# Later scaling and splitting of the output weight, an earlier first output tile, and re-timed first loads and text logits in a two-layer cross-attention kernel

## The reference

```python
# layer 0
q = split(x @ Wq.T); k, v = split(text @ Wk.T), split(text @ Wv.T)
k_ip, v_ip = split(ip @ Wk_ip.T), split(ip @ Wv_ip.T)
out = merge(attend(q, k, v)) + merge(attend(q, k_ip, v_ip))
x = out @ Wo.T + bo + x
# layer 1: its own weights, and one more term in the image scores
text_probs = softmax((q @ k_text.T) * scale)
sem = ((text_probs @ text) @ ip.T) * scale
ip_probs = softmax(scores + 0.5 * sem) * mask
x = (text_out + ip_out) @ Wout + bout + x
```

## Time and profile before

| | |
|---|---|
| median of 3 runs | 1746.2 us (1746.16 to 1747.57) |
| the profiled execution | 1748.87 us, of it span 1747.1 us |
| PE, DVE, ACT, POOL busy | 99%, 71%, 45%, 25% |
| HBM traffic | 133.96 MB read, 60.88 MB written, 112 GB/s |

### The profile page before, as it was taken

One profiled execution on the slowest core, in us unless ns is written; L12 is line 12 of the kernel. 1 busy time (PEld: TensorE's weight loads), 2 busy tenths in 40 slices (PEclk: granted clock), 3 DMA queues, 4 the chain that ended last, 5 costly groups with the idle time before them and its releaser, 6 DMA issues.

```text
span 1747.1 us, 52495 instructions
## 1 busy us (share of the span) xinstructions
PE 1727.5 (99%) x22178; PEld 1405.7 (80%) x22178; DVE 1241.9 (71%) x3112; ACT 781.2 (45%) x1579; POOL 441.9 (25%) x543
## 2 busy tenths in 40 slices
PE   8999999999999999999999999999999999999998
PEld 4778888888888888887577888888888888888875
DVE  6877676767677777676845567767676767677686
ACT  3334555554545454545322344534353445345343
POOL 3034333333342424223200112212121212122111
PEclk9999999999999999999999999999999999999999
DMA  8653535343434343435146232423142323224212
GB/s 327 128 158 115 161 117 154 113 135 113 135 110 139 109 136 112 139 108 200 61 88 175 64 97 75 117 75 96 48 136 53 116 65 119 62 83 109 82 45 70
DMA packets 124450, 198.45 MB, mean 114 GB/s; under 512 B 41928, under 2 KB 111064, under 8 KB 117496
## 3 DMA queue, kind: packets, MB, share of 16 engines
q1 hardware_dynamic: 118888, 168.95, 33.5%
q10 hardware_dynamic: 5328, 26.15, 4.0%
HBM read 133.96 MB, written 60.88 MB: 112 GB/s over the span
## 4 chain that ended last, share of the span: by engine, by line
PE 92%; DVE 4%; DMA 2%; ACT 1%; issue 1%; POOL 0%; SPq 0%; ACTq 0%; DVEq 0%
PE proj L597 65%; PE pv L752 6%; PE st L729 5%; PE rows L709 4%; PE rows L597 3%; PE proj L545 3%; PE proj L586 2%; PE rows L710 2%; DMA arena<-k_dram 1%; DMA raw<-text_dram 1%; PE rows L797 1%; ACT arena L1149 0%; PE rows L760 0%; DVE wparts L1508 0%; PE pv L661 0%
## 5 line engine op out<-in xcount | busy, mean ns | idle before, releaser
L597 PE MATMUL proj<-w_hl,cbuf 128*128 128x128 f16 x9600 | 600.9, 219 | 0.0
L597 PE MATMUL proj<-cbuf,w_hl 128*128 128x322 f16 (+1 forms) x3840 | 591.5, 300 | 0.4 <-DVE arena L1760 0.3
L597 PEld LDWEIGHTS proj<-w_hl,cbuf 128*128 128x128 f16 x9600 | 548.7, 98 | 2.3 <-issue 0.3
L597 PEld LDWEIGHTS proj<-cbuf,w_hl 128*128 128x128 f16 x3840 | 367.6, 97 | 163.7 <-DVE arena L1760 0.6
L1411 POOL TENSOR_TENSOR arena<-arena 128x400 f16<-128x400 f32 x240 | 231.1, 963 | 860.2 <-ACT arena L1149 860.2
L1148 ACT ACTIVATE arena<-st,rs 128x400 f16<-128x400 f32 x480 | 287.1, 598 | 259.3 <-DVE st L1886 155.2
L1124 ACT ACTIVATE arena<-proj 128x323 f16<-128x323 f32 (+1 forms) x160 | 70.6, 441 | 487.8 <-PE proj L597 487.8
L1149 ACT ACTIVATE arena<-st,rs 128x400 f32<-128x400 f32 x480 | 286.0, 596 | 0.0
L1805 DVE TENSOR_TENSOR arena<-arena 128x400 f16<-128x400 f32 x240 | 147.3, 614 | 95.7 <-ACT arena L1149 92.6
L752 PEld LDWEIGHTS pv<-arena 128*128 128x128 f16 x3840 | 175.2, 97 | 22.0 <-POOL arena L1411 0.8
L752 PE MATMUL pv<-arena 128*128 128x34 f16 (+3 forms) x3840 | 192.4, 189 | 0.5 <-POOL arena L1411 0.5
(11 more groups left out here) (202 smaller groups left out, 1675.6 us busy)
## 6 DMA issues: line engine op xcount, KB each, us to landing
arena<-k_dram SPq DMA_DIRECT2D x240, 185.2 KB, 3.6
k_dram<-arena SPq DMA_DIRECT2D x160, 161.2 KB, 1.9
raw<-ctx_dram SPq DMA_DIRECT2D x16, 1290.0 KB, 7.8
c_dram<-cbuf SPq DMA_DIRECT2D x16, 1290.0 KB, 6.7
cbuf<-c_dram SPq DMA_DIRECT2D x14, 1290.0 KB, 8.0
cbuf<-w_dram ACTq DMA_DIRECT2D x24, 640.0 KB, 8.2
arena<-q_dram SPq DMA_DIRECT2D x48, 125.0 KB, 2.6
w_hl<-w_dram ACTq DMA_DIRECT2D x8, 640.0 KB, 12.5
```

The costliest lines, as they stand in the source:

```text
L597: mm = nc.tensor.matmul(out, x[a](k), w[b](k), start=(k == 0 and m == 0), stop=(k == KT - 1 and m == 2))
```

## The change

It has six parts. (1) For the output weight, DVE's `turned_max` stays in the window g = 1 of the last batch but moves ahead of the second semantic tile, and `scale_chain` moves behind `prob_low(u, 2)`. (2) ACT's high parts move from g = 1 and 2 to g = 2 and 3. DVE's low parts 0 and 1 are made in g = 2, 2 and 3 in g = 3, and 4 in the last window, g = 4. (3) `out_tile(l, 0, 0)` is evicted by DVE before the third row maximum instead of behind it; in the last window DVE evicts tile 1 behind `prob_low(u, 0)` and tile 2 before `add_semantic(u, 3)`. (4) In `last_window` PE does `weigh(u, 0)` before score tile 3, and `out_tile(l, 0, 3)` begins after it. (5) In the preamble of layer 1 PE does `k_part(STEPS + 1, 1)` before `logits(0)`; ACT and DVE follow. (6) x comes in two pieces, both on SP; ACT waits for the first before it issues the rest of its loads, and issues the second weight's load after four evictions instead of two.

```diff
@@ -45,7 +45,7 @@
 QW = QK * C
 CH = KT * IP // 2
 TH = KT * TW // 2
-X_PIECES = ((0, 2), (2, 4), (4, CT))
+X_PIECES = ((0, 2), (2, CT))
 CB = 10400
 ORDER = (0, 2, 1, 3)
 TAIL_BANKS = (0, 1, 4)
@@ -187,7 +187,7 @@
 
         const_in, ready, sel_in = sem("const_in"), sem("ready"), sem("sel_in")
         x_in, wq_first, wq_in, wo_in = (sem("x_in0"), sem("x_in1")), sem("wq_first"), sem("wq_in"), sem("wo_in")
-        x_piece = tuple(sem(f"x_piece{n}") for n in range(3))
+        x_piece = tuple(sem(f"x_piece{n}") for n in range(2))
         wq_last = sem("wq_last")
         text_in, t_parts, t_chain, t_high, t_scaled = ((sem("text_in0"), sem("text_in1")), sem("t_parts"), sem("t_chain"), sem("t_high"),
                                                        sem("t_scaled"))
@@ -466,7 +466,7 @@
                         sp.wait_ge(v_full, 2 * (LAYERS * STEPS - G))
                         sp.dma_start(wo_raw, wo_d[1]).then_inc(wo_in, 16)
 
-            for n, (a, b) in enumerate(X_PIECES[0:2]):
+            for n, (a, b) in enumerate(X_PIECES):
                 sp.dma_start(x_first[:, a:b], x_d[0][:, a:b]).then_inc(x_piece[n], 16)
             sp.dma_start(wq[:, 3:], wq_d[0][:, 3:]).then_inc(wq_last, 16)
             sp.dma_start(raw[:, 0:TH], text_d[:, 0:TH]).then_inc(text_in[0], 16)
@@ -821,11 +821,10 @@
                 score_tile(u, 1)
                 out_tile(l, 0, 2, range(3, CT))
                 score_tile(u, 2)
-                out_tile(l, 0, 3, range(2))
+                weigh(u, 0)
                 score_tile(u, 3)
                 o_turn(u - 1)
-                out_tile(l, 0, 3, range(2, 4))
-                weigh(u, 0)
+                out_tile(l, 0, 3, range(4))
                 score_tile(u, 4)
                 out_tile(l, 0, 3, range(4, CT)), out_tile(l, 0, 4, range(1))
                 weigh(u, 1)
@@ -984,9 +983,9 @@
                 bank_done(pe, "vt", 1, TT - 1, c)
                 k_part(STEPS, c, 0, KT)
             k_part(STEPS + 1, 0, 0, KT)
+            k_part(STEPS + 1, 1, 0, KT)
             pe.wait_ge(pads, 2)
             logits(0)
-            k_part(STEPS + 1, 1, 0, KT)
             text_ip(0)
             odd_part(1, range(KT // 2))
             turn_probs(0)
@@ -1186,7 +1185,7 @@
                 n, k = u + 1, u + 2
                 more, more2 = exists(n, l), exists(k, l)
                 splits = iter(SLICES[4 * (g - 1):4 * g] if l == 0 and i < B - 1 and g in (1, 2) else ())
-                chunks = iter(((0, 1, 2, 3), (4,))[g - 1] if i == B - 1 and g in (1, 2) else ())
+                chunks = iter(((0, 1, 2, 3), (4,))[g - 2] if i == B - 1 and g in (2, 3) else ())
 
                 def split():
                     for k in splits:
@@ -1230,14 +1229,13 @@
                     k_unit(k, 0)
 
             act.dma_start(wq[:, 0], wq_d[0][:, 0]).then_inc(wq_first, 16)
-            a, b = X_PIECES[2]
-            act.dma_start(x_first[:, a:b], x_d[0][:, a:b]).then_inc(x_piece[2], 16)
+            act.wait_ge(x_piece[0], 16)
             act.dma_start(wq[:, 1:3], wq_d[0][:, 1:3]).then_inc(wq_in, 16)
             act.dma_start(raw[:, TH:], text_d[:, TH:]).then_inc(text_in[1], 16)
             load_weight(0, 0)
             q_tile(0, 0, 0), q_tile(0, 0, 1)
+            q_tile(0, 0, 2), q_tile(0, 0, 3)
             load_weight(0, 1)
-            q_tile(0, 0, 2), q_tile(0, 0, 3)
             act.wait_ge(t_chain, 5)
             for k in range(4):
                 split_text(k)
@@ -1316,8 +1314,8 @@
                 bank_done(act, "vt", 1, TT - 1, c)
             q_split(B)
             k_unit(STEPS, 0), k_unit(STEPS, 1)
+            k_unit(STEPS + 1, 0), k_unit(STEPS + 1, 1)
             logits(0)
-            k_unit(STEPS + 1, 0), k_unit(STEPS + 1, 1)
             odd_unit(1)
             act.wait_ge(pads, 2)
             turn_semantic(0)
@@ -1634,7 +1632,6 @@
 
             def wo_scale(l):
 
-                turned_max(os, "wo", l)
                 scale_chain(os, o_chain, 5 * l, os[:, 4:5], os[:, 5:6])
                 dve.wait_ge(tops, 2 * B + 2 * l)
                 nc.vector.tensor_scalar(oscale[:], ounit[:], os[:, 5:6], None, ALU.mult).then_inc(o_units, 1)
@@ -1906,7 +1903,7 @@
                     for _, c in zip(range(1 if l and count < 8 else count), wo_parts):
                         wo_part(l, c)
 
-                chunks = iter(((0, 1), (2, 3))[g - 1] if i == B - 1 and g in (1, 2) else ())
+                chunks = iter((2, 3) if i == B - 1 and g == 3 else ())
 
                 def low():
                     for c in lows:
@@ -1926,7 +1923,8 @@
                     normalise(u - 1)
                 if not more:
                     add_semantic(u, 1)
-                    out_tile(l, 0, 1)
+                if g == 1 and i == B - 1:
+                    turned_max(os, "wo", l)
                 if l == 0 and g == 1 and i < B - 1:
                     context_scale(i + 1)
                 if l == 0 and g == 2 and i < B - 1:
@@ -1938,17 +1936,21 @@
                 if more:
                     add_semantic(u, 1)
                 prob_low(u, 0)
-                if g == 1 and i == B - 1:
-                    wo_scale(l)
                 if ahead and g == 4:
                     semantic(i + 1)
                 low()
                 context_work(2)
                 if not more:
+                    out_tile(l, 0, 1)
+                add_semantic(u, 2)
+                if not more:
                     out_tile(l, 0, 2)
-                add_semantic(u, 2)
                 add_semantic(u, 3)
                 prob_low(u, 2)
+                if g == 1 and i == B - 1:
+                    wo_scale(l)
+                if not more:
+                    wo_low(l, 4)
                 if ahead and g == 2:
                     text_probs(i + 1)
                 context_work(2)
@@ -1961,6 +1963,8 @@
                     out_tile(l, 0, 3)
                 add_semantic(u, 5)
                 low()
+                if g == 2 and i == B - 1:
+                    wo_low(l, 0)
                 sooner = l and not (ahead and g == 3)
                 if more and sooner:
                     maxima(n, 0)
@@ -1978,10 +1982,10 @@
                     maxima(n, 1)
                     if more2:
                         k_unit(k, 0)
+                    else:
+                        out_tile(l, 0, 0)
                     maxima(n, 2)
                     context_work(1)
-                    if not more2:
-                        out_tile(l, 0, 0)
                     maxima(n, 3)
                     shift_parts(n)
                 context_work(8)
@@ -1990,7 +1994,7 @@
                 if i == B - 1 and g == 0:
                     wo_max(l)
                 if i == B - 1 and g == 2:
-                    wo_low(l, 4)
+                    wo_low(l, 1)
                 if g == 1 and i < B - 1:
                     q_split(r + 1)
 
@@ -2142,10 +2146,10 @@
             layer_scale(1)
             all_scales()
             k_unit(STEPS, 1)
+            k_unit(STEPS + 1, 0)
+            k_unit(STEPS + 1, 1)
             logits(0)
-            k_unit(STEPS + 1, 0)
             text_probs(0)
-            k_unit(STEPS + 1, 1)
             text_ip(0)
             probs_put(0)
             semantic(0)
```

## The result

The changed kernel takes 1752.1 us (median of 13 runs, 1749.41 to 1756.73), the kernel before 1746.99 beside it (13 runs, 1746.16 to 1748.67): a ratio of 1.0028, 95% interval 1.0020 to 1.0035. The profiled execution took 1752.93 us, its span is 1751.1 us.

The account below looks back on a forecast made before the run. PE's matmuls were taken to bound the kernel (1727.5 us, 99% of the span), so only its waits could change. Gains of 0.7, 1.0 and 2.1 less losses of 2.7 and 0.95 gave 1746.1 us, range 1743.8 to 1748.6.

Parts of the forecast that it names:

- the late load: Last window of layer 0: next query weight's load issued later, takes 6.6 us; PE stands 2.7 us (1.9 to 4.4).
- the logits: Preamble of layer 1: 0.68 us wait covered, but text_ip starts later; 0.95 us lost (0.7 to 1.3).
- the start: First loads: SP's text half lands about 1 us sooner; 0.7 us gained (0.1 to 1.6).
- The gain in g = 1: Last batch, window g = 1: PE's waits shrink; 1.0 us gained in layer 0, 2.1 in layer 1.
- The rival that VectorE becomes the bound there: Window g = 1: scale chain holds PE's projection, half of the 3.1 us given back; 1747.6 us, chance 13%.
- Windows g = 2 and 3: Last batch, ACT's moved high parts: zero cost, at most 0.4 us lost per layer.
- the first output tile: Evicted a maximum sooner by DVE: no effect, 0.3 us either way for both layers.
- The last window of layer 1: PE's block 4 waits for the low part, weigh(u, 0) fills another wait: zero, 0.3 us either way.
- the load collides: Layer change: load takes 8.3 us beside weight loads, PE stands 4.4; 1747.8 us, 8%; with slow clock about 1750.2, 5%.
- nothing moves: Start: small DMAs eat the text's lead, so nothing is gained there; 1746.8 us, chance 15%.
- the signs that were to show the prediction right: Changed profile: g = 1 at 17.4 to 17.7 us, later wq load and wait, text_ip wait about 1.5, text before 15.6.

Follow-up runs that it names:

- a2: The kernel before with only the changed first loads (part 6): 1749.72 us, ratio 1.0011 to the kernel before.
- c2: The kernel before with one edit, low part 4 of the output weight made in the last window: 1753.76 us, ratio 1.0035.
- c3: The kernel before with part 5 alone, both key projection parts ahead of the text logits: 1749.54 us, ratio 1.0013.
- a1: The changed kernel with its first loads as they were before (part 6 undone): 1752.31 us, ratio 1.0023 to the kernel before.
- d1: Changed kernel, parts 5 and 6 undone, low parts 2 and 3 in VectorE's gap in g = 3, part 4 where 3 stood, both layers: 1744.49 us.
- a3: The changed kernel with the fifth low part right behind the fourth, in g = 3: 1749.21 us, ratio 1.0007 to the kernel before.
- c1: Changed kernel, parts 5 and 6 undone, in layer 0 alone the fifth low part behind the last row maximum of g = 3: 1746.17 us.
- d2: d1 with x_late issued ahead of the mask's row on SyncE's queue: 1744.58 us, ratio 0.9984 to the kernel before.
- e1: d1 with layer 1's low parts where the changed kernel has them, so the gap is used in layer 0 alone: 1744.55 us, ratio 0.9982.
- c4: The changed kernel with SyncE's half of the text issued only when wq blocks 1 and 2 have landed: 1756.42 us, ratio 1.0055.
- a4: The changed kernel with the second key projection behind the logits again (part 5 undone): 1751.77 us, ratio 1.0021 to the kernel before.
- b2: The changed kernel with 16 dummy matmuls ahead of the wait for layer 1's query weight: 1753.02 us, ratio 1.0031 to the kernel before.
- b1: The changed kernel with 15 dummy matmuls after the first query tile at the start: 1751.66 us, ratio 1.0023 to the kernel before.
- b4: The changed kernel without ACT's wait for the first piece of x: 1753.79 us, ratio 1.0033 to the kernel before.

## Why the prediction was wrong

By the experiments, the sum should have read: start +1.6 (a2), g = 1 -1.14 and -2.35, the late load +6.0 (c2), the logits +1.7 (c3), g = 3 of layer 1 +0.3. That is 6.1, against 5.1 measured by the medians; the parts' runs agree with it within 1 us. The forecast had -0.7, -1.0 and -2.1, +2.7, +0.95 and 0. So 3.3 of the 6.3 us between the two sums stand at the late load and 2.3 at the start.

**The gain in g = 1: right.** 1.14 and 2.35 us in every kernel with the moved scale, against 1.0 and 2.1 (both just past the better bound, 1.1 and 2.3). The rival that VectorE becomes the bound there is shown wrong: both windows are 17.40 us long and PE is busy in all of it. No run separates the moved scale from the moved high parts.

**Windows g = 2 and 3, the first output tile: right at zero in three of four.** g = 2 takes 17.28 and 17.32 us. g = 3 costs 0.05 us in layer 0 and 0.30 in layer 1, inside the 0.4 that was allowed.

**The last window of layer 1: right at zero,** -0.03 us behind the last turn.

**The late load: the right mechanism, mis-sized.** The step that failed is "Without its 1.6 MB the weight loads have the queue to themselves earlier and are through when it starts, so I take 6.6", and with it the 2.7 us. The load took 7.9 us (7.3 to 8.5 in the eight profiles that issue it in the last window), and PE stood 3.80. The first half of that step held, near enough. ACT's last weight load landed at 826.08, 1.7 us behind the issue, but of ACT's queue only this row is left beside the load, 50 KB; DMA of the changed kernel from 824.3 to 832.3 us:

```profile
q10 hardware_dynamic: 15, 0.05, 1.4%
```

What failed is the 6.6, read from one transfer. The same trace holds a second load of 1600 KB with nothing on ACT's queue, `wo` of layer 1, and it took 7.2; in the sixteen profiles the two `wo` loads took 6.5 to 9.8 us, 26 of 32 of them 6.5 to 7.2. Why the late load took 7.9 stays open. And the sum had no clock in it: behind the 3.80 us the clock fell, 1.4 us more for the next four matmuls, up to 2.9 in a1. A wait of 3.80 and 1.4 for the clock are 5.2 us where 2.7 stood. The size is that of the rival "the load collides" with the clock, which had 5% and 1750.2 us (4.4 and 2 to 3 were reckoned); the collision that it names is 50 KB here. The rows of before did warn: the load that moves had itself taken 8.3, and the longest wait in that trace was too short to say anything about the clock behind a stall of 3 us.

**The logits: the right chain, the wrong base.** The 0.95 counted the 0.68 us wait of the profile of before as something that the new order saves. It stands in no other profile with the old order, and the cost against a usual run is 1.7.

**The start: the wrong sign.** The step that failed is "ACT's piece of `wq` may come 0.5 us either way, absorbed by the wait at 22.06". It came 2.3 us later, and the half clock behind the longer wait added 1.6. The waits at 22.06 and 26.94, 2.3 us together, took up what they could of these 3.9, and 1.6 were left. I had looked at the transfers that the hold favours, where the text came 3.4 us sooner and had been put at 1, and not summed those it holds back. The rival of this term, nothing moves, was wrong to the same side.

Of the signs that were to show the prediction right, all came: g = 1 at 17.40 us, a wait for the load under 5, the load 18 us later, 1.52 us ahead of `text_ip`, the text before 15.6. None of them looked at PE's wait for `wq` at the start or at the clock.

What stays open: the parts add up to 1 us more than the changed kernel's median; each kernel was timed with 5 to 13 runs that spread over 1 to 8 us, so this is not resolved. Of the changed kernel's 7.3 us in the layer change (6.50 + 0.83) the two waits and the half clock are 6.8 (3.80, 1.52 and 1.4). The rest is not traced; d1, which has neither wait, still has 0.2 of it. Nor is it shown which store makes ACT wait at 60 us in some executions.

## What to carry to other kernels

When a step moves, follow each transfer that hangs on it to its first use and subtract: the load here had 14 us to spare where it stood and 4 too few where it was put, and 1.6 MB wholly beside other loads took 9.3 to 10.7 us (a3, c1, d1, d2, e1), not 6.6. Price a long TensorE wait with the clock behind it, 1.4 to 2.9 us here, as a risk and not as a certainty. Before a wait in one profile is counted as a saving, see whether it stands in a second execution. A large stall can hide a good edit: with the old first loads and logits, and the low parts in VectorE's idle time, the rest of the change is 2.6 us faster than before (d1), where the whole was 5.1 slower.

## What the runs showed of the hardware

**The clock behind a wait.** PE's wait for `wq` at the start was followed by half clock where it was 1.98 to 2.15 us (a1, c2, c3, c4) and 2.9 to 4.1 (the changed kernel, a2, a3, a4 and b2, for about twice the time in a3 and b2), and not where it was 1.06 to 1.83 (before, c1, d1, d2, e1). So were the waits of 3.2 to 4.2 us at the layer change in the changed kernel, a1, a4, b1, b4 and c2. But the length of a wait does not decide alone. In c4 the wait there was 3.28 us, and the four matmuls behind it took 1.61. At the turn of the text's maxima PE waited 3.49 us in b4 and the clock stayed at 1.00; in c4 it waited 3.60 at the same place, and the clock was 0.50 behind it. What makes the difference is not shown. With the old first loads the waits for `wq` all end at 10.6 to 10.9 us, and they are longer where the first ten matmuls ran faster (3.57 us in c2, 4.25 in before), so they are not independent of the clock before them. Filling the wait with dummy matmuls kept the full clock (b1, b2). The Trainium skill, "TensorE: Matmul & The Clock Gate", section "What's actually happening", says that the clock stands at 1.2 GHz after idleness and returns to 2.4 by itself under load; the traces agree, with 0.50 granted behind these waits and 1.00 again after, but two long waits, in b4 and c4, were followed by no fall.

**Two queues share by packets, not by bytes.** DMA of the changed kernel from 9 to 10 us, where the text (SP's queue, q1) runs beside `wq` (ACT's, q10): packets, MB, share of 16 engines.

```profile
q1 hardware_dynamic: 27, 0.28, 66.5%
q10 hardware_dynamic: 28, 0.14, 34.3%
```

Equal packets, twice the bytes for the queue with the larger ones. The Trainium skill states in "DMA: Bandwidth & Descriptors", section "Queues, rings and completion order", that an engine alternates between its queues packet by packet, and the equal counts agree. Here, then, the load with the larger rows left the one with the smaller rows a third of the engines. And ACT's load, issued at 4.99, had nothing moved before 8.1 us; the queues from 5 to 8.1 us are this row alone:

```profile
q1 hardware_dynamic: 259, 1.32, 102.7%
```

SP's queue had all 16 engines there, with the rest of x, its 640 KB of `wq` and the first of the text. The hold put ACT's issue off from 1.67 to 4.99 us, by 3.3, and the landing by 2.3; with the text out of the way (c4) the landing was 0.5 later than before.
